# Attention scores of one sequence in six visits over four PSUM banks, value products in two cells, and one bank each for gate and up in the second half

## The chip, the cores and the metric

One NeuronCore of one Trainium2 chip runs the whole program. The metric is device time in microseconds (us) from the first to the last instruction of one execution; lower is better. Engines are named as the profile names them: PE (TensorE, matmul; PEld its weight loads), DVE (VectorE), ACT (ScalarE), POOL (GpSimd), SP (SyncE, which issues the DMAs).

## What is computed

Sixteen sequences of 256 tokens with 128 channels go through four residual blocks; all of it is fp32.

```python
x = L0_attn_a_x                                   # (16, 256, 128)
x = x + attn_a(layernorm(x))                      # linear attention: 32 heads of 4, a scan over tokens
x = x + ffn(layernorm(x))
x = x + attn_b(layernorm(x))                      # softmax attention, below
x = x + ffn(layernorm(x))                         # same weights again

def attn_b(x):                                    # 16 query heads of 8, one key and one value head
    q, k, v = x @ Wq + bq, x @ Wk + bk, x @ Wv + bv        # then rotary positions on q and k
    att = einsum('bthd,bThd->bhtT', q, k) / sqrt(8)
    att = softmax(where(causal, -inf, att))       # subtracts each row's maximum
    return einsum('bhtT,bThd->bthd', att, v).reshape(x.shape) @ Wo + bo

def ffn(x):                                       # sum over 8 experts, hidden width 512
    return sum(silu(x @ Wg[e]) * (x @ Wu[e]) @ Wd[e] for e in range(8))
```

## The kernel before

**Tiles, passes, units.** The 4096 tokens are 8 tiles of 512 (two sequences each). The feed-forward runs over all tiles twice, so there are 16 passes of 32 units, 512 units `n` in all. A unit is one expert's block of 128 hidden channels: `gate(n)`, `up(n)` and `down(n)` are three matmuls each of 512 columns (lines L855 to L857 of the helper `split_product`: high times high, high times low, low times high, in fp32r). ACT reads the gate bank (Silu in the units before `TANH` = 224, Tanh from there on, L684). From unit 224 on DVE then multiplies the gate into the tanh in `gated_half` (L1216, reads the gate bank again). DVE multiplies by the up bank in `hidden` (L1233), ACT rounds the product to HH (`hidden_hi`, L689), and POOL or DVE forms the rest HL (L525, L1222). `down(n)` runs three slots later and adds into one bank, `dbank`, for the 32 units of a pass.

**Slots.** Everything is placed on a common count of slots. In slot g PE runs gate(g), the side cells of point 0, up(g), the cells of point 1, down(g-3), the cells of point 2. The other engines walk over the same slots in program order: ACT does gate_act, hidden_hi of the slot before, then side work; DVE does gated_half, the maxima, a low part, hidden, then side work. Side work is the attention: block a for a tile is spread over some 48 slots beside the first half's passes, and block b (softmax attention) of tile t over 51 slots beside the second half's. In slots counted by `r` from a tile's first score visit, tile t's block b goes from r = -16 (its layer norm) to r = 35, and one tile follows the other every 32 slots, so that a lap of 32 slots holds each step of block b once. Where the unit does not exist (four slots between passes 8 and 9) only side work runs.

**Banks.** Before, three banks form a ring for gate and up (`fbank`: gate takes `2n % 3`, up `(2n+1) % 3`), `dbank` is one, two banks are `pair`, one is `single`, and `abank` takes block a's numerators and block b's value products. Tables `A_CELL` and `B_CELL` give each side cell its slot, point and bank. A cell waits until the cell that last used its bank has been read (`consumed`).

**Scores of one sequence.** Keys and queries are stacked in four row groups of 32 partitions (group g = 0 to 3), each with four heads j. First the row maxima: `rows`, six visits of two groups in the two banks of `pair`, with a matmul of 32 rows per group and head (L978, 128 columns; L987, 256 columns) and a causal mask added by a bf16 matmul into each bank (L981, L990); DVE reduces the two banks in one instruction (`maxima`, L1357, 128x1024). `split_maxima` (L1367, L1370) writes the maxima as weights, and `stack2` (L1074, L1076) adds them to the queries in the bank `single`; ACT copies it to Q2 (L804). Then `cols`, six visits with the transposed scores (L1005, or L1013 and L1021 with a wait between them, and masks L1008, L1017, L1024), which ACT turns into exponentials in PT, a ring of eight (`exps`, L766, 128x1024). `values` multiplies PT by v into `abank` in two halves of eight matmuls (L1035, L1041); ACT copies the result (L799), PE turns it (`sums`, L1050), DVE divides (L1379, L1382), and `ot` and `out` (L1057, L1065) project it.

The ring sets two waits in the second half, where PE may go one unit ahead:

```python
gate(n): after(pe, F.mul, n - 1)        # hidden(n-2) has read its up bank
up(n):   after(pe, F.sil, n); after(pe, F.half, n - TANH)   # gated_half(n-1) has read its gate bank
```

Of the kernel before, what the change touches and what calls it, by code (L numbers as in the profile page):

```python
# [14 lines left out]
P = 128  # L15
# [114 lines left out]
def unit_of(g):  # L130
# [17 lines left out]
for _b in range(SPT):
    for _i in range(6):
        B_CELL["rows", _b, _i] = (ROWS_AT[_b][_i], 0, None)  # L150
        B_CELL["cols", _b, _i] = (COLS_AT[_b][_i], 0, None)
BACK_CELL = (UNIT + LAG + 1, 2, 2)


def side_cells():
# [3 lines left out]
    def put(g, point, banks, key):  # L159
        for bank in (0, 1) if banks is None else (banks,):  # L160
            assert (g, point, bank) not in found, (g, point, bank, key)
            found[g, point, bank] = key
    for t in range(NT):
        for name, (r, point, bank) in A_CELL.items():
            put(a_slot(t) + r, point, bank, ("a", t, name))
        for name, (r, point, bank) in B_CELL.items():
            put(b_slot(t) + r, point, bank, ("b", t, name))
# [1369 lines left out]
```

## Time and profile before

| | us |
|---|---|
| median of 3 runs (lowest, highest) | 1717.82 (1716.12, 1718.82) |
| the profiled execution's own time | 1716.45 |
| its span, first to last instruction | 1714.7 |
| PE busy in it | 1574.8 (92%) |
| DVE, ACT, POOL busy | 1169.0, 892.6, 723.4 |
| passes 9 to 13 (one lap of block b each) | 113.0 each |
| pass 14 (end of the last tile's block b) | 100.1 |
| pass 15 (feed-forward alone) | 65.8 |

How to read it: a PE row's duration holds the time in which the matmul drains, so rows overlap, and the cost of a matmul is the distance between starts. A slot's length is the distance between the first gate matmuls of two units. "Idle before" is the time for which that engine had nothing to do, with what released it. PEclk is the share of full speed of TensorE's clock that was granted: 1.00 is 2.4 GHz, 0.50 is 1.2 GHz.

### The profile page before, as it was taken

What the parts mean: (1) busy time and instruction counts of PE and PEld (TensorE: products, weight loads), DVE (VectorE), ACT (ScalarE), POOL (GpSimd) and SP (SyncE); (2) the same over time, 40 slices, a digit from 0 to 9 for tenths busy, and PEclk for the clock granted to TensorE, in tenths of its full rate; (3) what the DMA queues carried; (4) which work ended last, traced back from release to release, by engine and by line L of the source; (5) the groups of instructions that cost most, each with busy time, mean ns of one, the idle gap of its engine ahead of it and who ended that gap; (6) DMA issues with size and microseconds to landing.
All of it is one profiled execution on the core that took longest, in us unless ns stands there. A gap on an engine that the chain in (4) does not pass through costs nothing.

```text
span 1714.7 us, 24047 instructions
## 1 busy us (share of the span) xinstructions
PE 1574.8 (92%) x7848; PEld 1136.2 (66%) x7848; DVE 1169.0 (68%) x1943; ACT 892.6 (52%) x1552; POOL 723.4 (42%) x663
## 2 busy tenths in 40 slices
PE   3488998899999999899999999999999999999998
PEld 2266777677767676675665766767667667576676
DVE  5678787878787869676674755746647557466465
ACT  2255555464646464546445564464554644645554
POOL 3647354534444434311033544444344444343365
PEclk9689999999999999999999999999999999999999
DMA  6314543333334434333222332422323323333353
GB/s 196 111 41 162 192 160 115 148 135 144 127 148 148 148 119 147 140 111 111 111 101 85 126 128 85 146 102 107 138 92 130 117 107 115 118 111 117 111 191 117
DMA packets 36239, 216.71 MB, mean 126 GB/s; under 512 B 3475, under 2 KB 17300, under 8 KB 19732
## 3 DMA queue, kind: packets, MB, share of 16 engines
q1 hardware_dynamic: 36116, 215.18, 34.7%
q8 instruction: 64, 1.05, 0.2%
q14 instruction: 59, 0.48, 0.1%
HBM read 200.49 MB, written 15.47 MB: 126 GB/s over the span
## 4 chain that ended last, share of the span: by engine, by line
issue 29%; POOL 20%; PE 1%; POOLq 0%; DVE 0%; ACT 0%; DVEq 0%
POOL HL L525 18%; POOL QK L597 1%; POOL X L588 0%; POOL RSTD_f L516 0%; POOL RSTD_in L516 0%; POOLq L190 0%; PE bank L855 0%; PE bank L857 0%; PE bank L856 0%; POOL VE_f L513 0%; POOL VE_in L513 0%; POOL NB_in L520 0%; POOL NM_f L518 0%; POOLq L196 0%; POOL NM_in L518 0%
## 5 line engine op out<-in xcount | busy, mean ns | idle before, releaser
L525 POOL TENSOR_TENSOR HL<-HF,HH 128x512 fp32r<-128x512 f32 x312 | 417.4, 1338 | 657.7 <-ACT HH L689 657.7
L1233 DVE TENSOR_TENSOR HF<-SG,bank 128x512 f32<-128x512 f32 x512 | 349.5, 683 | 172.7 <-PE bank L857 103.6
L855 PE MATMUL bank<-XTH,W 128*128 128x512 f32 x1024 | 434.4, 424 | 10.4 <-ACT SG L682 9.9
L857 PE MATMUL bank<-XTH,W 128*128 128x512 f32 x1024 | 403.8, 394 | 0.0
L1216 DVE SCALAR_TENSOR_TENSOR SG<-SG,bank 128x512 f32<-128x512 f32 x288 | 197.9, 687 | 301.3 <-ACT SG L684 300.6
L856 PE MATMUL bank<-XTL,W 128*128 128x512 f32 x1024 | 403.1, 394 | 0.0
L684 ACT ACTIVATE SG<-bank 128x512 f32<-128x512 f32 x288 | 172.3, 598 | 399.4 <-PE bank L857 397.8
L689 ACT ACTIVATE HH<-HF 128x512 fp32r<-128x512 f32 x512 | 319.7, 624 | 28.4 <-DVE HF L1233 27.6
L682 ACT ACTIVATE SG<-bank 128x512 f32<-128x512 f32 x224 | 133.6, 596 | 245.7 <-PE bank L857 244.4
L855 PEld LDWEIGHTS bank<-XTH,W 128*128 128x128 f32 x1024 | 194.8, 190 | 91.6 <-issue 29.8
L855 PE MATMUL bank<-HH,W 128*128 128x512 f32 x512 | 216.8, 423 | 14.6 <-DVE HL L1222 13.4
L857 PEld LDWEIGHTS bank<-XTH,W 128*128 128x128 f32 x1024 | 193.9, 189 | 43.6
L856 PEld LDWEIGHTS bank<-XTL,W 128*128 128x128 f32 x1024 | 195.1, 191 | 31.5
L857 PE MATMUL bank<-HH,W 128*128 128x512 f32 x512 | 202.5, 395 | 0.0
L856 PE MATMUL bank<-HL,W 128*128 128x512 f32 x512 | 201.5, 394 | 0.0
L1222 DVE TENSOR_TENSOR HL<-HF,HH 128x512 fp32r<-128x512 f32 x200 | 165.6, 828 | 0.0
L855 PEld LDWEIGHTS bank<-HH,W 128*128 128x128 f32 x512 | 97.2, 190 | 48.3 <-DVE HL L1222 16.8
L1357 DVE TENSOR_REDUCE NM<-pair 128x4 f32<-128x1024 f32 (+1 forms) x96 | 117.0, 1218 | 3.1 <-PE pair L981 2.1
L1269 DVE TENSOR_TENSOR_SCAN S<-BETA,KV 128x512 f32<-128x512 f32 x80 | 117.9, 1479 | 0.1
L857 PEld LDWEIGHTS bank<-HH,W 128*128 128x128 f32 x512 | 97.0, 189 | 22.2
L856 PEld LDWEIGHTS bank<-HL,W 128*128 128x128 f32 x512 | 97.4, 190 | 15.1
L562 POOL TENSOR_TENSOR S<-S,PQ 128x512 f32<-128x512 f32 x40 | 62.4, 1562 | 96.6 <-DVE S L1269 96.6
(237 smaller groups left out, 1850.0 us busy)
## 6 DMA issues: line engine op xcount, KB each, us to landing
W<-kept_w SPq DMA_DIRECT2D x120, 1536.0 KB, 6.5
kept_w<-W SPq DMA_DIRECT2D x8, 1536.0 KB, 6.2
X<-in_L_attn_a_x_dram SPq DMA_DIRECT2D x8, 256.0 KB, 5.5
WS<-in_L_ffn_Wg_dram SPq DMA_DIRECT2D x8, 256.0 KB, 6.5
WS<-in_L_ffn_Wu_dram SPq DMA_DIRECT2D x8, 256.0 KB, 6.8
WS<-in_L_ffn_Wd_dram SPq DMA_DIRECT2D x8, 256.0 KB, 7.2
out_dram<-X SPq DMA_DIRECT2D x8, 256.0 KB, 7.2
CST<-in_tables_dram SPq DMA_DIRECT2D x1, 896.5 KB, 5.2
```

The costliest lines, as they stand in the source:

```text
L525: g.tensor_tensor(HL[:, n % HRING, :], HF[:, n % HFRING, :], HH[:, n % HRING, :].bitcast(F32), ALU.subtract).then_inc(F.hl, 1)
L682: act.activation(SG[:, n % 2, :], fbank[2 * n % 3], ACT.Silu).then_inc(F.sil, 1)
L684: act.activation(SG[:, n % 2, :], fbank[2 * n % 3], ACT.Tanh, scale=0.5).then_inc(F.sil, 1)
L689: act.activation(HH[:, n % HRING, :], HF[:, n % HFRING, :], ACT.Copy).then_inc(F.hh, 1)
L855: pe.matmul(dst, wh, xh, start=start, stop=False)
L856: pe.matmul(dst, wh, xl, start=False, stop=False)
L857: return pe.matmul(dst, wl, xh, start=False, stop=stop)
L1216: v.scalar_tensor_tensor(gated, gated, 1.0, fbank[2 * n % 3], ALU.add, ALU.mult).then_inc(F.half, 1)
L1222: v.tensor_tensor(HL[:, n % HRING, :], HF[:, n % HFRING, :], HH[:, n % HRING, :].bitcast(F32), ALU.subtract).then_inc(F.hlv, 1)
L1233: v.tensor_tensor(HF[:, n % HFRING, :], gated, fbank[(2 * n + 1) % 3], ALU.mult).then_inc(F.mul, 1)
L1269: v.tensor_tensor_scan(S[:, m, c, :], BETA[:, m, :], KV[:, c, :], 0.0, ALU.mult, ALU.add).then_inc(A.scan, 1)
L1357: v.tensor_reduce(dst, src, AX.X, ALU.max, negate=True).then_inc(B.row_used, 1)
```

## The change

The eight PSUM banks are named anew: `gubank` (two), `quad` (four, next to each other), `dbank`, `abank`. In the first half the ring of three is kept (two banks of `gubank` and bank 0 of `quad`); from unit 224 on gate has one bank and up the other. A side cell may now lie in `quad` 0 to 3 or in `abank` (4). `rows` and `cols` make three visits per sequence each, all four groups at once, two slots apart and at point 2. Each visit ends with two pairs of masks, and signals after each pair; DVE takes one half (two banks) in the visit's slot and one in the next, ACT both halves in the next slot. `maxima` stands behind `hidden` in DVE's order. The value products of one head pair become one cell of sixteen matmuls. The stack goes from `single` to banks 0 and 1 of `quad`, both halves in one slot. Block b's layer norm starts five slots earlier (r = -21), and its turn is at r = -18.

```diff
-ROW_PAIRS = [(0, 1), (2, 3), (4, 6), (5, 7), (8, 10), (9, 11)]
-PT_RING = 8
-          ("stack", 0, 0): (8, 1, 2), ("stack", 0, 1): (9, 1, 2), ("stack", 1, 0): (14, 1, 2),
-          ("stack", 1, 1): (15, 1, 2), ("sums", 0, 0): (20, 1, 2), ("sums", 0, 1): (21, 1, 2),
-          ("ot", 0): (22, 1, 2), ("out", 0): (23, 1, 2), ("sums", 1, 0): (27, 1, 2), ("sums", 1, 1): (27, 2, 1),
-          ("ot", 1): (28, 1, 2), ("out", 1): (29, 1, 2), "fturn": (33, 2, 2)}
-ROWS_AT = [[6 * b + i for i in range(6)] for b in range(SPT)]
-COLS_AT = [[12 + 6 * b + i for i in range(6)] for b in range(SPT)]
+          ("stack", 0, 0): (7, 1, 0), ("stack", 0, 1): (7, 2, 1), ("stack", 1, 0): (13, 1, 0),
+          ("stack", 1, 1): (13, 2, 1), ("pv", 0, 0): (16, 1, 4), ("pv", 0, 1): (18, 1, 4), ("sums", 0, 0): (20, 1, 4),
+          ("sums", 0, 1): (21, 1, 4), ("pv", 1, 0): (22, 1, 4), ("pv", 1, 1): (24, 1, 4), ("ot", 0): (25, 1, 0),
+          ("out", 0): (26, 1, 0), ("sums", 1, 0): (26, 2, 4), ("sums", 1, 1): (27, 1, 0), ("ot", 1): (28, 1, 4),
+          ("out", 1): (29, 1, 4), "fturn": (33, 1, 4)}
+ROWS_AT = [[0, 2, 4], [6, 8, 10]]
+COLS_AT = [[12, 14, 16], [18, 20, 22]]
...
+        gubank = ctx.enter_context(nc.psum_tensor("gubank", [P, 2, 512], F32))[:, :, :]
+        quad = ctx.enter_context(nc.psum_tensor("quad", [P, 4, 512], F32))[:, :, :]
+        fbank = [gubank[:, 0, :], gubank[:, 1, :], quad[:, 0, :]]
+        sbank = [*[quad[:, i, :] for i in range(4)], abank]
+        def gate_bank(n):
+            return fbank[2 * n % 3] if n < TANH else fbank[0]
...
-            return {"rows": lambda: (B.row_used, 6 * n + name[2] + 1),
-                    "cols": lambda: (B.t_used, 6 * n + name[2] + 1),
+            return {"rows": lambda: (B.row_used, 6 * n + 2 * name[2] + 2),
+                    "cols": lambda: (B.t_used, 6 * n + 2 * name[2] + 2),
+                    "pv": lambda: (B.os, 2 * n + name[2] + 1),
...
             def exps(n, i):
-                m = 6 * n + i
-                act.wait_ge(B.t_ready, m + 1)
-                act.activation(PT[:, at:at + 2, :], pair, ACT.Exp, scale=DB ** -0.5).then_inc(B.t_used, 1)
+                for h in range(2):
+                    act.wait_ge(B.t_ready, 6 * n + 2 * i + h + 1)
+                    act.activation(PT[:, at:at + 2, :], quad[:, 2 * h:2 * h + 2, :], ACT.Exp,
+                                   scale=DB ** -0.5).then_inc(B.t_used, 1)
...
             def gate(n):
-                after(pe, F.mul, n - 1)
+                if n > TANH:
+                    pe.wait_ge(F.half, n - TANH)
+                else:
+                    after(pe, F.mul, n if n == TANH else n - 1)
             def up(n):
-                after(pe, F.sil, n)
-                after(pe, F.half, n - TANH)
+                if n > TANH:
+                    pe.wait_ge(F.mul, n)
+                else:
+                    after(pe, F.sil, n)
...
             def rows(t, b, i):
+                if i == 0:
+                    for j in range(NJ):
+                        for g in range(NG):
+                            pe.matmul(quad[:, g, j * P:(j + 1) * P], q[g][:, j, 0:P], ks[g][:, 0:P], start=(j == 0),
...
+                for h in range(2):
+                    for g in (2 * h, 2 * h + 1):
...
+                    m.then_inc(B.row_ready, 1)
...
+            def values(n, b, z, dst):
+                pe.wait_ge(B.t_used, 6 * n + 2 * z + 4)
...
             for slot in range(G_FIRST, G_LAST + 1):
-                for t, r in b_tiles(slot):
-                    for b in range(SPT):
-                        if r in ROWS_AT[b]:
-                            maxima(t, b, ROWS_AT[b].index(r))
...
                     hidden(n)
+                for t, r in b_tiles(slot):
+                    for b in range(SPT):
+                        for i, at in enumerate(ROWS_AT[b]):
+                            if r in (at, at + 1):
+                                maxima(SPT * t + b, b, i, r - at)
```

The places in the order of the instructions on which the prediction rests are three. In these rows `gubank`, `dbank` and `quad` (before: `bank`, `pair`, `single`) are banks, XTH and XTL the feed-forward's input, HH and HL its hidden product, QST, KST and Q_86 (Q2) the stacked queries and keys, NMP the maxima, PT the exponentials, and the names in brackets the semaphores waited for.

PE, slots r = 6 and 7 of a tile in the middle, the change: the first score visit of the second sequence at the end of slot 6, gate and up of slot 7, the first stack.

```order
L999 MATMUL quad<-KST,QST 128x128 [waits b_row_used]
L999 MATMUL quad<-KST,QST 128x128 x15
L1009 MATMUL quad<-MASKB 128x512 x4
L873 MATMUL gubank<-XTH,W 128x512 [waits f_half]
L874 MATMUL gubank<-XTL,W 128x512
L875 MATMUL gubank<-XTH,W 128x512
L873 MATMUL gubank<-XTH,W 128x512 [waits f_mul]
L874 MATMUL gubank<-XTL,W 128x512
L875 MATMUL gubank<-XTH,W 128x512
L1077 MATMUL quad<-QST,SELR 128x256 [waits b_nml,b_row_used]
L1079 MATMUL quad<-SELR,NMP 128x128 x2
```

The stack's bank is one that the score visit of the slot before filled, so the stack waits for `row_used`, the maxima of both halves. Before, the same place of PE (slot r = 8) had the stack in a bank of its own:

```order
L987 MATMUL pair<-KST,QST 128x256 [waits b_row_used]
L987 MATMUL pair<-KST,QST 128x256 x3
L990 MATMUL pair<-MASKB 128x2x128 x2
L855 MATMUL bank<-XTH,W 128x512 [waits f_half,f_sil]
L856 MATMUL bank<-XTL,W 128x512
L857 MATMUL bank<-XTH,W 128x512
L1074 MATMUL single<-QST,SELR 128x256 [waits b_nml,nf_lo]
L1076 MATMUL single<-SELR,NMP 128x128 x2
```

There the waits are for the split maxima and for a read that lies far back, and the score visit stands between gate and up instead of behind down.

ACT, slots r = 13 to 15 of the same tile, the change: the last instruction of hidden_hi in slot 13, then all side work of that slot and the next two.

```order
L707 ACTIVATE HH<-HF 128x512 [waits f_down,f_mul]
L783 ACTIVATE PT<-quad 128x1024 [waits b_pv,b_t_ready] x2
L822 ACTIVATE Q_86<-quad 128x512 [waits b_t_ready,b_q2_ready] x2
L693 ACTIVATE XN<-X,NB_in,RSTD_in 128x128 [waits nin_nb,nin_tp]
L693 ACTIVATE XN<-X,NB_in,RSTD_in 128x128 x3
L702 ACTIVATE SG<-gubank 128x512 [waits f_mul,f_gate]
L707 ACTIVATE HH<-HF 128x512 [waits f_down,f_mul]
L727 ACTIVATE XH<-abank 128x512 [waits b_v_ready,a_proj,nin_tp]
L702 ACTIVATE SG<-gubank 128x512 [waits f_mul,f_gate]
L707 ACTIVATE HH<-HF 128x512 [waits f_down,f_mul]
L783 ACTIVATE PT<-quad 128x1024 [waits b_pv,b_t_ready] x2
```

Two exponentials, two copies of the stack and the next tile's normalisation, which before were spread over the slots r = 12 to 18, stand in one slot now, ahead of the next slot's tanh (L702).

DVE, slots r = 11 and 12, the change: gated_half, hidden, the second half of the last maxima, the next tile's statistics, and the split of the second sequence's maxima.

```order
L1218 SCALAR_TENSOR_TENSOR SG<-SG,gubank 128x512 [waits f_sil]
L1235 TENSOR_TENSOR HF<-SG,gubank 128x512 [waits f_up,f_half,f_hl]
L1357 TENSOR_REDUCE NM<-quad 128x2x2 [waits b_row_ready,b_nml]
L1204 BN_STATS ST_in<-X 128x6 [waits nin_mv,f_done]
L1204 BN_STATS ST_in<-X 128x6 x3
L1208 BN_AGGR MV_in<-ST_in 128x2 [waits nin_nm,nin_st]
L1208 BN_AGGR MV_in<-ST_in 128x2 x3
L1218 SCALAR_TENSOR_TENSOR SG<-SG,gubank 128x512 [waits f_sil]
L1235 TENSOR_TENSOR HF<-SG,gubank 128x512 [waits f_up,f_half,f_hl]
L1367 CAST NMP<-NM 128x4x4 [waits b_q2_ready,b_row_used]
```

The maxima stand behind hidden, which itself waits for up of the same slot, and the statistics have come five slots forward to stand behind the maxima.

## Rows read from the trace of the kernel before

**Rows 1.** The page, part 1: busy time, share, instructions of PE and others
```profile
PE 1574.8 (92%) x7848; PEld 1136.2 (66%) x7848; DVE 1169.0 (68%) x1943; ACT 892.6 (52%) x1552; POOL 723.4 (42%) x663
```
**Rows 2.** Windows: a lap of block b, then pass 15; busy by engine, PEclk, DMA
```profile
1087.90:1200.90 113.00, 111.20 (x606) 75.83 (x604) 68.59 (x120) 60.59 (x105) 48.38 (x43) 1.00 0.32 115
...
1641.00:1706.80 65.80, 65.67 (x292) 54.03 (x290) 44.66 (x65) 36.29 (x66) 41.34 (x33) 1.00 0.45 164
```
**Rows 3.** Timeline of PE, three gates, two score visits between them (start, duration, engine, line)
```profile
1089.53 0.39 PE L855 MATMUL bank<-XTH,W 128*128 128x512 f32 x1
...
1090.30 0.50 PE L987 MATMUL pair<-KST,QST 32*128 32x256 f32 x4
...
1092.35 0.39 PE L855 MATMUL bank<-XTH,W 128*128 128x512 f32 x1
...
1095.54 0.39 PE L855 MATMUL bank<-XTH,W 128*128 128x512 f32 x1
```
**Rows 4.** Timeline of PE, around transposed scores (to 1119.89) and value products
```profile
1112.05 0.39 PE L855 MATMUL bank<-XTH,W 128*128 128x512 f32 x1
...
1114.87 0.39 PE L855 MATMUL bank<-XTH,W 128*128 128x512 f32 x1
...
1118.15 0.39 PE L857 MATMUL bank<-XTH,W 128*128 128x512 f32 x1
...
1119.89 0.39 PE L856 MATMUL bank<-XTL,W 128*128 128x512 f32 x1
...
1121.82 1.06 PE L1035 MATMUL abank<-PT,VF 128*32 128x512 f32 x8
...
1126.55 0.64 PE L1041 MATMUL abank<-PT,VF 128*32 128x256 f32 x8
```
**Rows 5.** Timeline of pass 15: a gate, its tanh, its gated_half, the next gate
```profile
1681.35 0.39 PE L855 MATMUL bank<-XTH,W 128*128 128x512 f32 x1
...
1682.23 0.60 ACT L684 ACTIVATE SG<-bank 128x512 f32<-128x512 f32 x1 [0.92 <-PE bank L857]
...
1682.86 0.69 DVE L1216 SCALAR_TENSOR_TENSOR SG<-SG,bank 128x512 f32<-128x512 f32 x1 [0.57 <-ACT SG L684]
...
1683.39 0.39 PE L855 MATMUL bank<-XTH,W 128*128 128x512 f32 x1
1683.64 0.69 DVE L1233 TENSOR_TENSOR HF<-SG,bank 128x512 f32<-128x512 f32 x1
```
**Rows 6.** Timeline of DVE: gated_half, maxima, hidden back to back
```profile
1093.86 0.69 DVE L1216 SCALAR_TENSOR_TENSOR SG<-SG,bank 128x512 f32<-128x512 f32 x1 [0.41 <-ACT SG L684]
1094.46 1.22 DVE L1357 TENSOR_REDUCE NM<-pair 128x8 f32<-128x1024 f32 x1
1095.60 0.68 DVE L1233 TENSOR_TENSOR HF<-SG,bank 128x512 f32<-128x512 f32 x1
```
**Rows 7.** Timeline of ACT: tanh, HH, an exponential; then one normalisation
```profile
1115.75 0.60 ACT L684 ACTIVATE SG<-bank 128x512 f32<-128x512 f32 x1 [0.79 <-PE bank L857]
1116.25 0.62 ACT L689 ACTIVATE HH<-HF 128x512 fp32r<-128x512 f32 x1
1116.77 1.02 ACT L766 ACTIVATE PT<-pair 128x1024 f32<-128x1024 f32 x1
...
1137.42 1.64 ACT L675 ACTIVATE XN<-X,NB_in,RSTD_in 128x128 f32<-128x128 f32 x4
```
**Rows 8.** Timeline: a product that had waited, DVE's ropes ahead of it
```profile
1165.84 1.40 DVE L1396 SCALAR_TENSOR_TENSOR B<-pair,BQK,CST 128x512 f32<-128x512 f32 x2
...
1166.64 0.50 PE L855 MATMUL pair<-XH,WBH 128*128 128x512 f32 x1 [0.77 <-DVE B L1396]
```
**Rows 9.** Timeline of PE in the first half, around two of its waits
```profile
633.38 0.50 PE L855 MATMUL bank<-XTH,W 128*128 128x512 f32 x1 [1.41 <-ACT SG L682]
...
635.52 0.63 PE L892 MATMUL single<-CST,XNF 128*128 128x128 f32 x4 [1.17 <-ACT XNF L675]
```
**Rows 10.** Windows of those waits; PEclk is the third number from the end
```profile
633.00:640.00 7.00, 5.46 (x18) 4.17 (x19) 3.85 (x7) 5.62 (x12) 0.29 (x2) 0.76 0.02 7
```

More of the change, by code:

```diff
@@ new lines, with back_cell, bank_of @@
+ROWS_AT = [[0, 2, 4], [6, 8, 10]]
+COLS_AT = [[12, 14, 16], [18, 20, 22]]
+for _b in range(SPT):
+    for _i in range(3):
+        B_CELL["rows", _b, _i] = (ROWS_AT[_b][_i], 2, None)
+        B_CELL["cols", _b, _i] = (COLS_AT[_b][_i], 2, None)
+BACK_CELL = (UNIT + LAG + 1, 2, 3)
+BACK_LATE = (UNIT + LAG + 1, 1, 4)
+def back_cell(s):
+    return BACK_CELL if s < NT - 2 else BACK_LATE
+def bank_of(key):
+    if key[0] == "back":
+        return back_cell(key[1])[2]
+    if key[0] == "a":
+        return A_CELL[key[2]][2]
+    if key[1:] == (0, "turn"):
+        return 3
+    return B_CELL[key[2]][2]
@@ L155, in side_cells, with put @@
 def side_cells():
     found = {}
[L159 to L162, printed above, removed]
+    def put(g, point, key):
+        bank = bank_of(key)
+        for at in range(4) if bank is None else (bank,):
+            assert (g, point, at) not in found, (g, point, at, key)
+            found[g, point, at] = key
     for t in range(NT):
[L164 to L167, printed above, removed]
+        for name, (r, point, _) in A_CELL.items():
+            put(a_slot(t) + r, point, ("a", t, name))
+        for name, (r, point, _) in B_CELL.items():
+            put(b_slot(t) + r, point, ("b", t, name))
@@ L983, in rows @@
                 else:
[L984 removed]
                     for j in range(2):
[L986 to L987 removed]
+                        for g in range(NG):
+                            pe.matmul(quad[:, g, j * SEQ:(j + 1) * SEQ], q[g][:, 2 * (i - 1) + j, P:SEQ], ks[g],
                                       start=(j == 0), stop=False, skip_group_check=True)
[L989 to L991 removed]
@@ new lines, in cols @@
+                for h in range(2):
+                    for g in (2 * h, 2 * h + 1):
+                        if i == 0:
+                            m = pe.matmul(r3(quad[:, g, :], NJ), MASKB[:, 2, :], spread(MASKB[:, 1, :], NJ),
+                                          start=False, stop=True, skip_group_check=True)
+                        else:
+                            m = pe.matmul(r3(quad[:, g, :], 2)[:, :, 0:P], MASKB[:, 2, :], spread(MASKB[:, 1, :], 2),
+                                          start=False, stop=True, skip_group_check=True)
+                    m.then_inc(B.t_ready, 1)
@@ new lines, in values @@
+            def values(n, b, z, dst):
+                pe.wait_ge(B.t_used, 6 * n + 2 * z + 4)
+                for g in range(NG):
+                    pe.matmul(dst[g * RG:(g + 1) * RG, :], VF[:, 2 * b, :], PT[:, NG * (z + 1) + g, :],
+                              start=True, stop=False, skip_group_check=True)
+                for g in range(NG):
+                    x = pe.matmul(r3(dst[g * RG:(g + 1) * RG, :], 2)[:, :, P:SEQ], VF[:, 2 * b + 1, :],
+                                  r3(PT[:, g, z * SEQ:(z + 1) * SEQ], 2), start=False, stop=True,
+                                  skip_group_check=True)
@@ L1132, in side @@
             def side(slot, point):
-                for t, r in b_tiles(slot):
-                    for b in range(SPT):
-                        for z in range(2):
-                            first = COLS_AT[b][3 * z + 2]
-                            if r in (first, first + 1) and point == 2:
-                                values(SPT * t + b, b, z, r > first)
                 for t, r in a_tiles(slot):
@@ L1481, in _ @@
                     gated_half(n)
-                for t, r in b_tiles(slot):
-                    for b in range(SPT):
-                        if r in ROWS_AT[b]:
-                            maxima(t, b, ROWS_AT[b].index(r))
                 old = unit_of(slot - 2)
```

234 lines of the change are left out of this document (91 added, 143 removed).

## The prediction

> **What bounds it now.** I read the page's busy times first, then the windows of single laps, then the timeline of PE inside a lap, because a mean over the span mixes the two halves. On the page PE leads with 92% [rows 1]. In a lap of block b it is busy for 111.2 of 113.0 us, while DVE has 68.6, ACT 60.6 and POOL 48.4 [rows 2]; the one long wait of PE is for DVE's ropes, 0.77 us in front of a product [rows 8], with a second like it. So in these laps PE's own work is the time, and in the last pass too (65.7 of 65.8). What is to be seen in the timelines is what a slot is made of. Without side work, gate to gate is 2.04 us [rows 5]: nine matmuls of 512 columns at 0.23. A slot with a small score visit (four matmuls of 256 columns, two masks) takes 2.82, with a large one (eight of 128 columns, two masks of 512) 3.19 [rows 3]. A first or second visit of the transposed scores gives 2.82 as well; the third takes 1.74 between two matmuls that are 0.45 apart without it, so 1.29 [rows 4]. A visit of 0.78 holds 0.23 of scores and 0.24 of masks; the other 0.3 is going into 32-row matmuls and out again.
>
> **What PE saves.** Per sequence the visits cost 2 x 1.15 + 4 x 0.78 = 5.4 for the maxima and 4 x 0.78 + 2 x 1.29 = 5.7 for the exponentials [rows 3, 4]. Four groups instead of two have no row. The two of a pair start together (the four instructions of the small visit occupy 0.50 in all [rows 3]), so the lower bound is that four cost what two do, plus two more masks; the upper is that the other two run after the first, 0.5 more per visit. I take the lower, since what is known is that groups of rows overlap, and keep the other for the range. Then the large visit is 1.15 + 2 x 0.23 = 1.6, the small 0.78 + 2 x 0.12 = 1.02, the first of the exponentials (four masks of 512) 0.78 - 0.24 + 4 x 0.23 = 1.45, the others 1.02: 3.6 and 3.5. The values' matmuls stay (1.06 and 0.64 per head pair [rows 4]); one cell for two saves one change of mode, 0.3, twice a sequence. Sum: 11.1 - 7.1 + 0.6 = 4.6 per sequence, 9.2 per lap.
>
> For this one step the Trainium skill has another figure: TensorE: Matmul & The Clock Gate, "Measured speedup vs the span model", gives four row tiles of 512 columns 3.07 times the speed of one, not four. By that, as an estimate, four would take 1.3 times as long as one, 0.1 to 0.15 more in each of 12 visits, some 12 us in the whole sum. No row here shows four groups at once.
>
> **What the ring of two adds.** A gate now waits for gated_half of the unit before. In pass 15 the tanh starts 0.88 after the gate's first matmul and gated_half 0.63 after that; it lasts 0.69 [rows 5]. So it ends 2.20 after the gate began, 0.16 later than the next gate begins today. A PE product released by DVE starts 0.05 after it and then takes 0.11 longer (0.50 instead of 0.39) because its weights load only then [rows 8]. So a slot without side work becomes 2.04 + 0.16 + 0.05 + 0.11 = 2.36. In pass 15 that is **32 x 0.32 = 10.3 us**, with no cover. Up waits for hidden, which starts 0.78 after gated_half and ends 0.73 after the gate it has released could start [rows 5]: about when PE gets there, so no further cost.
>
> **New waits in a lap**, counted from the gate's start in a slot; PE reaches the first side cell 1.36 after it (six matmuls).
> - Slot 7, stack behind the maxima of the visit one slot before. The tanh ends at 1.5, and until 1.6 DVE has the first half of these maxima, 1.13 to the next instruction [rows 6], and the split; gated_half and hidden follow (0.78 and 0.60 to the next instruction [rows 5, 6]), and the second half of the maxima, 1.22, ends at 4.2. PE waits **2.85**. Queued behind it are a down and the second stack, and with PE everyone.
> - Slot 13, stack behind two exponentials. Tanh starts at 0.88, HH 0.50 later, the exponentials 0.52 and 0.9 after that, and the second ends 1.02 later [rows 7], at 3.82. PE waits **2.5**.
> - Slot 14, turn of the next tile. ACT first copies two stacks (some 0.6 each, like the tanh), the second only when PE has made it, and then normalises for 1.64 [rows 7]: 2.35 after the slot's start against 1.36. **1.0**.
> - Slots 15 to 24. The value cells and the next q wait for exponentials that end at 3.82 of the slot before, or for the copy after them at 4.3; PE, after a short slot of 2.25, arrives at 3.7. Pair by pair the loss over PE's work is 0.5, 1.0, 0.35, 0 and 0.5: **2.3**.
> - Light slots 3, 5, 9 and 11, whose own gate did not wait, take 2.25 (no late weights) and push the next up by 0.1; DVE's extra work in slots 2, 8 and 11 delays three gates: **1.8**.
>
> Together 10.4. The two waits for ropes are partly filled, since out and sums now stand in slots 25 and 26 where PE idled: -1.4. A lap becomes 113.0 - 9.2 + 10.4 - 1.4 = 112.8. The 1.8 us that PE idled have become more than 10, and nothing is gained.
>
> **The rest.** The first lap (pass 7) has DVE form most of the low parts, 0.6 more per slot in front of hidden, and the gates now wait on DVE: +3. In pass 14, which has no next tile to prepare, the ten slots from 25 on are nearly bare and become up to 0.3 longer, less what the missing turn saves: +1.5. The change of rings at unit 224 costs one drained slot: +1. The first half keeps ring and places: 0. POOL's and SP's work is the same; the low parts have three slots of room and the weights load by passes. Six laps: -1. Sum: -1 + 3 + 1.5 + 1 + 10.3 = **+15**.
>
> **The clock.** The granted clock is 1.00 (2.4 GHz) in the lap and in pass 15 [rows 2]. In the first half PE waited 1.41 and then 1.17 us within 3.3 us [rows 9], and over 7 us the mean is 0.76 [rows 10], which is 3.4 us at 1.2 GHz; of six places like it three show this. Slots 7 and 13 with 14 wait longer than that, 16 times in all. If half of them bring such a stretch, each costs at most 1.7 us of PE's work: at most 14, and less behind slot 14, where ACT sets the pace. I take 7.
>
> Against the profiled execution's own 1716.45: 1716.45 + 15 + 7 = 1738.5, so **1738 us**; that execution lies 1.4 under the median of the runs, which is well inside the error. Its own range is 1724 to 1755: the laps' ten waits may each be off by some tenths, times seven laps, and the clock between 0 and 14.
>
> **Rivals.**
> - *PE's saving stays, the waits don't come* (faster). The place is the stacks and the turn in slots 7, 13 and 14, 6.3 us a lap. If DVE and ACT have read the banks when PE gets there, seven and a half laps lose 47 us less: 1691. For it: DVE idles 44 us of a lap, ACT 52 [rows 2]. Against it: both walk their queue in order, and the instruction waited for stands behind hidden or HH of the same slot. It decides at 2.8 us a lap: with less than 3.5 left of the 6.3 the change gains.
> - *Four groups don't overlap.* 12 visits x 0.5 x 7.5 laps = 45 at most; half of them hide in waits that exist anyway: +25, 1763. Against it the pairs that start together [rows 3].
> - *The clock falls at most of the 16 places, for longer.* Twice 14 instead of 7: 1759.
> - *It cancels*: pass 15 costs less than 10 and the laps gain 2 each: 1716 to 1721. That needs two errors of one sign.
>
> **Chances.** Forecast 0.52, PE's saving stays 0.19, no overlap 0.10, clock 0.10, cancels 0.09. A measurement of this kernel tells about 0.2%, 3.4 us, from no change. Faster by more 0.18, within it 0.09, slower 0.73. The range that leaves out 2 in 10 goes from 1700, which takes in the upper part of the first rival, to 1772.
>
> **What would show it.** Right: pass 15 near 76 us with gates 2.36 apart; PE's stack rows (L1077) with idle 2 to 3 us released by DVE's maxima (L1357) in slot 7 and by ACT's exponentials in slot 13; laps of 111 to 115. The four matmuls of a first exponential visit starting together, and taking no longer up to their masks than a pair did, would confirm the saving. Wrong: laps under 110 (waits absent), laps over 117 (groups in series, or PEclk well under 1.00 in the laps), or pass 15 still at 66.

## The result and the profile after

The changed kernel takes 1754.32 us (median; 1753.22 to 1765.98) against 1717.55 for the kernel before: ratio 1.022, 95% interval 1.0193 to 1.0247. It is slower by some 2%, as forecast (1738, range 1700 to 1772), and 16 us slower than the number given. The profiled execution took 1753.62, with a span of 1751.8, 37.1 over that of before.

The page of the changed kernel, part 1, answers to [rows 1]: PE has 17 us less to do in a span that is 37 us longer.

```profile
PE 1557.5 (89%) x7720; PEld 1115.4 (64%) x7720; DVE 1177.6 (67%) x1943; ACT 883.5 (50%) x1552; POOL 723.5 (41%) x663
```

Windows of the changed kernel: pass 7, pass 10 (a lap as in [rows 2]), pass 14, pass 15. Columns: stretch, length, busy time of PE, PEld, DVE, ACT, POOL, then PEclk, DMA share, GB/s.

```profile
740.80:870.60 129.80, 112.33 (x589) 75.81 (x589) 89.17 (x145) 59.99 (x102) 16.09 (x18) 0.96 0.28 101
1104.90:1219.70 114.80, 106.80 (x589) 73.61 (x587) 69.06 (x121) 59.39 (x104) 48.23 (x44) 0.99 0.31 115
1562.00:1667.20 105.20, 97.63 (x518) 65.79 (x516) 60.08 (x102) 53.81 (x92) 42.66 (x37) 0.98 0.33 119
1667.20:1743.90 76.70, 76.37 (x294) 49.70 (x292) 44.62 (x65) 36.37 (x65) 41.28 (x33) 1.00 0.38 140
```

The windows of passes 7 and 14 in the kernel before:

```profile
736.40:853.60 117.20, 113.30 (x603) 77.42 (x603) 82.44 (x145) 60.83 (x102) 16.08 (x17) 0.99 0.30 112
1540.90:1641.00 100.10, 99.32 (x532) 68.02 (x531) 58.36 (x101) 54.59 (x93) 42.62 (x36) 1.00 0.35 125
```

In the lap PE's idle time goes from 1.8 us [rows 2] to 8.0. The 37.1 us by passes, each from the end of the last `hidden` of one to that of the next: pass 0 +1.5, pass 6 +2.9, **pass 7 +12.6**, pass 8 -0.7, passes 9 to 13 together +4.9, pass 14 +5.1, **pass 15 +10.9**; passes 1 to 5 are equal within 0.1. Passes are counted from 0, so the four slots without a unit lie between passes 7 and 8. In the kernel before pass 13 takes 114.1 and not 113.0 like its neighbours, since a half-speed stretch of the clock stands in it (from 1513.3).

**The visits.** PE's timeline in the lap, around a large visit, a first visit of the exponentials, and a small one (start, duration, engine, line, count):

```profile
1094.24 0.39 PE L875 MATMUL dbank<-HH,W 128*128 128x512 f32 x1
1094.56 0.67 PE L999 MATMUL quad<-KST,QST 32*128 32x128 f32 x16
1095.16 1.04 PE L1009 MATMUL quad<-MASKB 128*128 128x512 bf16 x4
1095.85 0.59 PE L873 MATMUL gubank<-XTH,W 128*128 128x512 f32 x1
1096.27 0.39 PE L874 MATMUL gubank<-XTL,W 128*128 128x512 f32 x1
...
1135.31 0.51 PE L1025 MATMUL quad<-Q,KST 32*128 32x512 f32 x4
1135.74 1.04 PE L1029 MATMUL quad<-MASKB 128*128 128x512 bf16 x4
...
1146.16 0.40 PE L875 MATMUL dbank<-HH,W 128*128 128x512 f32 x1
1146.48 0.51 PE L1025 MATMUL quad<-Q,KST 32*128 32x512 f32 x4
1146.92 0.61 PE L1032 MATMUL quad<-MASKB 128*128 128x256 bf16 x4
1147.29 0.48 PE L873 MATMUL gubank<-XTH,W 128*128 128x512 f32 x1
1147.61 0.40 PE L874 MATMUL gubank<-XTL,W 128*128 128x512 f32 x1
```

From the last matmul of a down to the second of the next gate is 2.03 us over the large visit and 1.45 over the small, where two bare intervals of 0.227 would be 0.45: the visits cost 1.58 and 1.00 (predicted 1.6 and 1.02). The four matmuls of 512 columns start together and occupy 0.51, with the masks 0.43 behind their start. In the kernel before two of them had these same numbers:

```profile
1112.82 0.50 PE L1005 MATMUL pair<-Q,KST 32*128 32x512 f32 x2
1113.25 0.39 PE L1008 MATMUL pair<-MASKB 128*128 128x256 bf16 x2
```

**The stall in slot 7.** DVE, and then PE, in slots 6 and 7 of pass 10; the gate of slot 7 starts at 1113.28:

```profile
1113.31 1.22 DVE L1357 TENSOR_REDUCE NM<-quad 128x8 f32<-128x1024 f32 x1 [0.43 <-PE quad L1009]
1114.45 0.25 DVE L1367 CAST NMP<-NM 128x16 fp32r<-128x16 f32 x2
1114.73 0.29 DVE L1370 TENSOR_TENSOR NMP<-NM,NMP 128x16 fp32r<-128x16 f32 x2
1115.01 0.69 DVE L1218 SCALAR_TENSOR_TENSOR SG<-SG,gubank 128x512 f32<-128x512 f32 x1
1115.79 0.69 DVE L1235 TENSOR_TENSOR HF<-SG,gubank 128x512 f32<-128x512 f32 x1
1116.39 1.22 DVE L1357 TENSOR_REDUCE NM<-quad 128x8 f32<-128x1024 f32 x1
```

```profile
1117.66 0.39 PE L1077 MATMUL quad<-QST,SELR 128*128 128x256 f32 x1 [2.63 <-DVE NM L1357]
```

Read it downwards: first half of the maxima, split, gated_half, hidden, second half, and only then the stack. That is the queue the prediction wrote down, 0.2 us shorter. The three longest waits of PE in this lap (engine, tile, line, what it waited for; us, times, longest):

```profile
PE quad L1077 <- DVE NM L1357: 2.6, 1, 2.6
PE quad L1077 <- ACT PT L783: 2.3, 1, 2.3
PE abank L915 <- ACT XN L693: 0.9, 1, 0.9
```

**The ring of two.** The chain in pass 15, a gate, its tanh, its gated_half, the next gate, answers to [rows 5]:

```profile
1692.98 0.50 PE L873 MATMUL gubank<-XTH,W 128*128 128x512 f32 x1
...
1693.99 0.60 ACT L702 ACTIVATE SG<-gubank 128x512 f32<-128x512 f32 x1 [1.26 <-PE gubank L875]
...
1694.62 0.69 DVE L1218 SCALAR_TENSOR_TENSOR SG<-SG,gubank 128x512 f32<-128x512 f32 x1 [0.91 <-ACT SG L702]
...
1695.45 0.47 PE L873 MATMUL gubank<-XTH,W 128*128 128x512 f32 x1
```

Gates stand 2.47 apart here and 2.40 in the mean of the pass (2.36 predicted, 2.04 before).

**The clock.** Windows of the stall in slot 7 and of the stretch behind it (columns as above):

```profile
1114.00:1118.80 4.80, 2.17 (x13) 1.60 (x12) 3.48 (x8) 1.32 (x3) 1.27 (x1) 1.00 0.69 287
1118.80:1122.20 3.40, 3.40 (x13) 2.92 (x12) 0.00 (x0) 1.00 (x3) 0.00 (x0) 0.51 0.00 0
```

For 3.4 us the granted clock is 0.51 (the 1.2 GHz level). One such stretch stands in each of passes 9 to 14, in turn behind slot 13 and slot 7; pass 8 has both stalls and no stretch. That prices it, since the slots are otherwise alike: where it stands behind slot 7 the slots 7 and 8 take 7.28 and 4.29, without it 6.50 and 3.48, 1.6 together; where it stands behind slot 13 that slot takes 6.70 instead of 6.11, 0.6, and slot 14 no longer (4.57 for 4.54), as PE's wait of 0.86 for ACT falls away there. Passes 9 to 14 hold three of each: 6.6 us. Without them a lap is 113.2 us (predicted 112.8).

### The profile page after: what moved, and what is told of

Its sections match the earlier page's. It is cut to its first block and busy times, and to the rows that moved or that the text cites. A ratio compares the mean times of both kernels' runs of the same rounds, so it can differ in the third digit from the quotient of the medians.

```text
span 1751.8 us, 23526 instructions
## 1 busy us (share of the span) xinstructions
PE 1557.5 (89%) x7720; PEld 1115.4 (64%) x7720; DVE 1177.6 (67%) x1943; ACT 883.5 (50%) x1552; POOL 723.5 (41%) x663
## 3 DMA queue, kind: packets, MB, share of 16 engines
q8 instruction: 62, 1.02, 0.2%
## 5 line engine op out<-in xcount | busy, mean ns | idle before, releaser
L1218 DVE SCALAR_TENSOR_TENSOR SG<-SG,gubank 128x512 f32<-128x512 f32 x288 | 197.2, 685 | 349.3 <-ACT SG L702 349.0
L873 PE MATMUL gubank<-XTH,W 128*128 128x512 f32 x875 | 379.9, 434 | 26.2 <-DVE HF L1235 7.8
L702 ACT ACTIVATE SG<-gubank 128x512 f32<-128x512 f32 x288 | 172.9, 600 | 424.9 <-PE gubank L875 424.9
L1235 DVE TENSOR_TENSOR HF<-SG,gubank 128x512 f32<-128x512 f32 x438 | 300.0, 685 | 119.3 <-PE gubank L875 56.6
L874 PE MATMUL gubank<-XTL,W 128*128 128x512 f32 x875 | 347.8, 398 | 0.0
L875 PE MATMUL gubank<-XTH,W 128*128 128x512 f32 x875 | 347.6, 397 | 0.0
L873 PEld LDWEIGHTS gubank<-XTH,W 128*128 128x128 f32 x875 | 167.8, 192 | 132.0 <-DVE HF L1235 37.7
L873 PE MATMUL dbank<-HH,W 128*128 128x512 f32 x512 | 220.3, 430 | 12.9 <-DVE HL L1224 11.9
L875 PE MATMUL dbank<-HH,W 128*128 128x512 f32 x512 | 203.7, 398 | 0.0
L874 PE MATMUL dbank<-HL,W 128*128 128x512 f32 x512 | 202.4, 395 | 0.0
L875 PEld LDWEIGHTS gubank<-XTH,W 128*128 128x128 f32 x875 | 167.2, 191 | 38.3
L874 PEld LDWEIGHTS gubank<-XTL,W 128*128 128x128 f32 x875 | 168.4, 192 | 22.6
L700 ACT ACTIVATE SG<-gubank 128x512 f32<-128x512 f32 x149 | 88.9, 596 | 160.1 <-PE gubank L875 159.3
L873 PEld LDWEIGHTS dbank<-HH,W 128*128 128x128 f32 x512 | 97.5, 191 | 58.6 <-issue 26.0
L875 PEld LDWEIGHTS dbank<-HH,W 128*128 128x128 f32 x512 | 97.4, 190 | 22.1
```

Of the source, the lines that this page charges most:

```text
L700: act.activation(SG[:, n % 2, :], gate_bank(n), ACT.Silu).then_inc(F.sil, 1)
L702: act.activation(SG[:, n % 2, :], gate_bank(n), ACT.Tanh, scale=0.5).then_inc(F.sil, 1)
L873: pe.matmul(dst, wh, xh, start=start, stop=False)
L874: pe.matmul(dst, wh, xl, start=False, stop=False)
L875: return pe.matmul(dst, wl, xh, start=False, stop=stop)
L1218: v.scalar_tensor_tensor(gated, gated, 1.0, gate_bank(n), ALU.add, ALU.mult).then_inc(F.half, 1)
```

## The experiments

The theory is the prediction's: PE's saving is real, and the time is lost in waits that come from where the cells stand (stacks in the quad, the turn, one bank each for gate and up). The rivals: the stalls are slack of a chain through ACT and DVE; the clock is the loss; the order on DVE is of no account.

**e1_half_wait.** The stacks stand in banks 0 and 1, which the first half of a visit has read.

```diff
-                        after(pe, *consumed(old))
+                        sem, count = consumed(old)
+                        first = bank_of(key) in (0, 1) and old[0] == "b" and old[2][0] in ("rows", "cols")
+                        after(pe, sem, count - 1 if first else count)
```

> A stack in bank 0 or 1 of the quad waits only for the first half of the visit before it (first half of the maxima, first exponential), no longer for both halves. Theory (the two stacks' waits are the lap's loss): the idle time at L1077 in slot 7 goes from 2.63 to about 0.4 us (the split of the maxima of slot 6 is what is left), in slot 13 from 2.27 to about 1.25; 3.2 us a lap, eight laps, so 1754 - 26 = 1728; if the half-speed stretches, one a lap now, go with the shorter waits, up to 1.7 us a lap more, 1714. Rival (the chain through ACT and DVE sets the lap, PE's time in the stalls is slack): the time comes back in slots 8 to 12 and 14 to 24, 1746 to 1754. Second rival (the clock alone is the loss): waits shorter, but the gain is only where a half-speed stretch goes, at most 15 us, and laps without one keep 113 to 115 us.

Measured: **1712.28**, 0.9955 [0.9938, 0.9972] of before. The wait in slot 7 is 0.13, that in slot 13 as in this list of a lap's waits, with the lap's window:

```profile
PE quad L1077 <- ACT PT L783: 1.3, 1, 1.3
```

```profile
1084.80:1194.40 109.60, 105.04 (x589) 72.36 (x587) 69.05 (x122) 59.39 (x104) 48.25 (x44) 1.00 0.33 118
```

A lap gets 4.1 to 5.2 us shorter: 3.4 of waits, and the clock, which stays at 1.00 in passes 9 to 14. Over the profiled span of 1708.1 the laps of passes 9 to 13 give back 22.7 of 43.7 us, passes 6 and 7 another 10. The stalls were no slack, and the waits are the larger part; the clock goes with them.

**e2_stack_abank.**

```diff
-("stack", 0, 0): (7, 1, 0), ("stack", 0, 1): (7, 2, 1), ("stack", 1, 0): (13, 1, 0), ("stack", 1, 1): (13, 2, 1)
+("stack", 0, 0): (9, 1, 4), ("stack", 0, 1): (10, 1, 4), ("stack", 1, 0): (13, 1, 4), ("stack", 1, 1): (15, 1, 4)
```

> The four stacks move out of the quad into the fifth bank, to slots 9, 10, 13 and 15, so that they wait for no half of a visit. Theory (the stacks' place in the quad is the loss): 2.63 and 2.27 us a lap go, and up to 1 comes back, since the turn of the next tile in slot 14 and the stack in slot 15 now follow each other in one bank: 4 a lap, 32 in all, 1722; with the half-speed stretches gone too, 1707. Rival (ACT's and DVE's queues set the lap): 1745 or more, and the idle time shows up in front of the scores of slots 12 and 18 or the value products instead.

Measured: **1704.17**, 0.991 [0.9887, 0.9934], below what the theory gave even with the clock. The lap, and the longest wait left in it:

```profile
1086.50:1195.00 108.50, 104.52 (x589) 72.43 (x587) 69.03 (x122) 59.16 (x104) 48.29 (x44) 1.00 0.32 119
```

```profile
PE abank L915 <- ACT XN L693: 1.6, 1, 1.6
```

With the stacks elsewhere the quads beat the pairs by 4.5 us a lap (108.5 against 113.0). PE's waits in slots 7 and 13 are gone, and the turn in slot 14 takes 0.7 of it back.

**e3_ring_last.**

```diff
+            return ... fbank[0] if n < LAST else fbank[2 * (n - LAST) % 3]
...
-                if n > TANH:
+                if TANH < n <= LAST:
                     pe.wait_ge(F.half, n - TANH)
```

> From the last pass on, gate and up go round three banks again (the quad's first bank is the third). Theory (the chain gate, tanh, gated half, gate with one bank each costs 0.32 us a slot): the last pass falls from 76.7 to 66 to 67 us, 1754 - 10 = 1744, all other passes as they were. Rival (something else that came with the change, such as later low parts or weights, sets the last pass): 73 us or more there, 1750 to 1754.

Measured: **1748.14**, 1.0173 [1.014, 1.0206]. In the profile the last pass:

```profile
1668.20:1734.40 66.20, 66.10 (x294) 54.37 (x292) 44.63 (x65) 36.35 (x65) 41.32 (x33) 1.00 0.45 162
```

66.2 against 76.7, 65.8 before: all but 0.4 of pass 15's excess is the ring. The median gains 6 and not 10, with the four runs between 1744 and 1752. The profiled execution, the fastest of them, gains 9.5: there passes 13 and 14, which the edit does not touch, take 3.6 more, with a longer half-speed stretch in each, and pass 0 takes 2.4 less.

**e8_before_ring2.** The same from the other side: the kernel before, with gate and up in one bank each from the second half on, and the waits of the change for it.

```diff
-                after(pe, F.mul, n - 1)
+                if n > TANH:
+                    pe.wait_ge(F.half, n - TANH)
+                else:
+                    after(pe, F.mul, n if n == TANH else n - 1)
```

> The kernel before with one thing of the change: in the second half gate and up have one bank each, with the waits that this needs. Theory (the chain alone costs 0.32 us in each slot without side work, and little where a slot is 2.8 us or longer): the last pass goes from 65.8 to 76 us, a lap of block b by 0 to 3 us (up waits for the product, which there stands behind the maxima on DVE): 1728 to 1748, most likely 1732. Rival (the ring costs only together with the new places of the side work): last pass under 70, 1717 to 1722.

Measured: **1728.99**, 1.0061 [1.0046, 1.0076], 10 us more. The last pass:

```profile
1642.30:1719.00 76.70, 76.30 (x294) 49.69 (x292) 44.61 (x66) 36.37 (x65) 41.25 (x33) 1.00 0.38 141
```

10.9 there, 2.1 in pass 14, and 0.0 in the laps of passes 9 to 12, where each takes 113.0 as before. So with the side work where it was before, the chain costs only in slots that hold little but their unit.

**e4_pool_pass7.**

```diff
-            return n >= NT * UNIT or n % UNIT in POOL_LOW
+            return n >= TANH or n % UNIT in POOL_LOW
```

> In pass 7 all low parts are formed on POOL, as in the passes after it, instead of most of them on DVE. Theory (the 0.86 us low parts on DVE in front of the product make the gates and ups of pass 7 wait, and make its two stalls 4.1 and 3.7 instead of 2.6 and 2.3): pass 7 falls from 129.8 to 118 to 121 us, 1754 - 10 = 1744. Rival (pass 7 is long by its three half-speed stretches, 5 us, whatever DVE does): 125 us or more in pass 7, 1749 to 1754.

Measured: **1745.86**, 1.0153 [1.0124, 1.0182]. Pass 7 falls from 129.8 to 117.5. In the changed kernel its longest waits of PE are these:

```profile
PE gubank L873 <- DVE HF L1235: 7.2, 9, 1.3
PE quad L1077 <- DVE NM L1357: 4.1, 1, 4.1
PE quad L1077 <- ACT PT L783: 3.7, 1, 3.7
```

The nine for hidden become one of 1.3, and the 4.1 becomes 2.6. The 3.7 stays, against the theory: what makes it longer than the 2.3 of other laps is in the main a row of ACT, 1.28, that stands in front of its first exponentials and in no later lap:

```profile
796.53 1.28 ACT L783 ACT_TABLE_LOAD   x1
```

The kernel before has it too (at 776.88). Pass 8 takes 3.5 more, with two half-speed stretches that it did not have; the rest of the gain stays. The size fits, but the reason is not settled by it. The trace of the changed kernel shows what a wait of 1.28 is made of, POOL and DVE and then PE:

```profile
754.35 1.29 POOL L543 TENSOR_TENSOR HL<-HF,HH 128x512 fp32r<-128x512 f32 x1 [5.77 <-ACT HH L707]
754.39 1.79 DVE L1224 TENSOR_TENSOR HL<-HF,HH 128x512 fp32r<-128x512 f32 x1
...
756.10 0.67 DVE L1235 TENSOR_TENSOR HF<-SG,gubank 128x512 f32<-128x512 f32 x1
...
756.83 0.50 PE L873 MATMUL gubank<-XTH,W 128*128 128x512 f32 x1 [1.28 <-DVE HF L1235]
```

DVE's low part begins 0.04 after POOL's and lasts until 0.54 after POOL's has ended. Seven of DVE's 26 low parts in pass 7 are like this, 1.61 to 1.79 long; eighteen others take 0.68, and one 1.39, beside a sum of 128x512 on POOL (L615). The kernel before has one (1.81); six others begin there 1.17 behind POOL's and take 0.68. The next run takes POOL's away instead.

**e12_dve_pass7.**

```diff
-            return n >= NT * UNIT or n % UNIT in POOL_LOW
+            return n >= NT * UNIT or n < TANH and n % UNIT in POOL_LOW
```

> The opposite of the run with POOL's low parts: in pass 7 all low parts are formed on DVE, none on POOL. In the changed kernel's trace seven of DVE's 26 low parts in pass 7 take 1.6 to 1.8 us, each of them beside a low part on POOL that began within 0.3 us of it; eighteen of the other nineteen take 0.68. Theory (the two engines' low parts hold each other up, and the seven collisions are what makes pass 7 long): with none on POOL all take 0.68, though there are six more of them; the waits of 1.3 for the product go, and pass 7 falls from 129.8 to about 121, 1754 - 9 = 1745. Rival (DVE simply has too much to do in pass 7, and each low part in front of the product counts): six more low parts make it longer, 131 to 135, 1756 to 1759.

Measured: **1748.02**, 1.0163 [1.0134, 1.0192]. With 33 low parts on DVE instead of 26, pass 7 is 7.2 us **shorter** (122.6). The group of low parts on DVE in pass 7 (count, busy us, mean ns, idle before):

```profile
L1224 DVE TENSOR_TENSOR HL<-HF,HH 128x512 fp32r<-128x512 f32 x33 | 23.4, 710 | 0.0
```

The ten waits for hidden that are left are 0.2 each. Slot by slot, the five slots that had held such a wait lose 0.9 to 1.1 each and the two stalls 1.1 and 0.4. So 7.2 of pass 7's 12.6 is not DVE's amount of work, but that the two engines' low parts begin together. The amount is not free either: e4, where POOL forms them, has 117.5, and ten slots are some 0.4 shorter there than here. In each of the two steps, from the changed kernel to this run and from this run to e4, pass 7 also has 3.4 us less at half speed.

**e5_turn_back.** The turn goes back to `(-13, 1, 4)`, with statistics, normalisation and its two readers five slots later too.

> The next tile's normalisation and turn go back five slots later, to where the kernel before had them (turn in slot 19 of the lap, not 14), in the same bank; the stacks stay. Theory (the earlier normalisation costs 0.86 us in slot 14 and, for the first tile of block b, lands between block a's scans): pass 6 goes back from 95.8 to about 93, and the 0.86 in slot 14 goes; in slot 19 up to 1.0 comes, because the turn then follows the copy of the value cell of slot 18 in its bank: 1754 - 3 = 1751, at best 1744. Rival (the place of the turn is nothing): pass 6 stays at 95 to 96, 1754.

Measured: **1759.3**, 1.0233 [1.0209, 1.0256]: 5 us worse, where 3 to 10 better were expected. Pass 6 does fall, to 92.2. But the turn now follows the copy of a value cell in its bank, and the sums follow the turn and wait 0.3 for its copy (the first of these waits in pass 10):

```profile
PE abank L915 <- ACT OS L817: 1.0, 1, 1.0
```

1.3 for 0.9, and in passes 10, 11 and 14 twice the time at half speed, in pass 12 none. The expected 1.0 came; the second wait and the clock had been left out.

**e6_stack_turn.** From e2: turn at `(-17, 1, 4)`, stack (1, 1) at `(17, 1, 4)`.

> As the run with the stacks in the fifth bank, with the turn of the next tile one slot later (15, its normalisation still begun in 13) and the second sequence's second stack in slot 17. Theory (PE waits 1.59 us in slot 14 only because ACT has two exponentials and a stack's copy ahead of the normalisation): the wait goes, laps from 108.5 to about 107, 1704 - 11 = 1693. Rival (ACT is late for all of slots 13 to 18): the time comes back in front of the value products of slots 16 and 18 or of the scores of slot 18, 1700 to 1704.

Measured: **1736.98**, 1.0105 [1.009, 1.012], a miss by 44 us. The wait for XN is gone, and three others have come:

```profile
PE abank L1077 <- ACT OS L817: 2.8, 1, 2.8
PE gubank L873 <- DVE SG L1218: 1.4, 2, 1.0
PE abank L1040 <- DVE XL L1212: 1.0, 1, 1.0
```

The turn (15), a value cell (16), the stack (17) and a value cell (18) now follow each other in one bank, a slot apart. The value cell of 16 waits 1.0 for the turn's copy (XL), which the rival had; the stack of 17 waits 2.8 for the value cell's copy (OS), which ACT makes a slot later, behind that slot's unit. The lap is 112.9, with a half-speed stretch again. Neither theory had the 2.8. In e2 too the bank is used in the slots 13 to 16 running, but slot 17 behind the value cell is free: that was the slack.

**e7_all.** e6 with the edits of e3 and e4.

> The run before this one, with the ring of three in the last pass and POOL's low parts in pass 7. Theory (the costs lie in different passes and add up): 10.4 less in the last pass, about 6 less in passes 7 and 8 together, 1693 - 16 = 1677. Rival (POOL's low parts in pass 7 only push the cost into pass 8, where the run with that edit alone had 3.4 more): 1682 to 1690.

Measured: **1721.07**, 1.0011 [1.0, 1.0022]. It starts from e6's 1737, not from 1693, and ends where the kernel before stands, but the difference is what was expected, 15.9; in the profiles: 10.5 in pass 15 and 9.3 in pass 7, 1.4 given back in pass 8.

**e9_sum.** e2 with the edits of e3 and e4.

> The stacks in the fifth bank in slots 9, 10, 13 and 15, the ring of three in the last pass and POOL's low parts in pass 7, with the turn left in slot 14. Theory (the three costs lie in different passes and add up): 1704 - 10.4 (last pass) - 5 (pass 7, which still has 122 there against 117 before) = 1689, faster than the kernel before by 1.7%. Rival (POOL's low parts in pass 7 only move the time into pass 8): 1694.

Measured: **1688.92**, 0.9822 [0.9806, 0.9839]. The costs add up. Pass 7 is 112.8 (117.2 in the kernel before, 122.2 in e2), pass 15 66.2. Pass 8 gives 2.9 of pass 7's 9.4 back, as the rival had it for all of the 5.

**e10_norm_early.** From e9: statistics, scale and normalisation of the next tile one slot earlier (`r == -22`, `-21` and `-20`), the turn where it was.

> As the run with the sum, with the next tile's statistics, scale and normalisation one slot earlier (12 for ACT, which has no exponentials there), the turn still in slot 14. Theory (PE waits 1.59 us there for a normalisation that stands behind two exponentials and a copy on ACT): the wait goes down to about 0.3, which the copy of the stack in the same bank keeps; 1.3 a lap, 7 laps, 1689 - 9 = 1680. Rival (what is ahead of the turn in its bank is as late as the normalisation, or pass 6 gets longer by as much): 1687 to 1692.

Measured: **1676.61**, 0.9748 [0.9734, 0.9763], 2.5% faster than the kernel before. The wait for XN is gone; the statistics, now in DVE's slot 10, delay gated_half of slot 11 and with it the gate of slot 12 by 0.9, in the first row of the lap's waits:

```profile
PE gubank L875 <- DVE SG L1224: 1.6, 2, 0.9
```

So a lap gains only 0.8 to 1.0, some 4 of the 12 us in all. Passes 6 to 8 give 6, and lose three half-speed stretches (at 725, 790 and 862 us in e9); the rest is in passes 4 and 5, which the edit does not touch. That the number came out below the theory's 1680 is thus partly luck.

**e11_maxima_first.** The changed kernel with `maxima(...)` again ahead of `hidden_lo` and `hidden` in DVE's loop.

> The changed kernel with DVE's order of before: in each slot the maxima ahead of the low part and the product. Theory (with two banks the next up waits for the product, so the maxima of a visit that stands at the slot's end must be behind it): about 1.2 us more in each of the six slots after a visit of the maxima, 0.6 less at the stack of slot 7; 6 a lap, 1754 + 45 = 1799. Rival (the order on DVE is indifferent, since it idles 45 us a lap): 1750 to 1758.

Measured: **1788.93**, 1.0402 [1.0387, 1.0418]. A lap is 119.5, and among its waits are:

```profile
PE gubank L873 <- DVE HF L1235: 7.1, 8, 1.1
...
PE quad L1077 <- DVE NM L1357: 1.3, 1, 1.3
```

Eight ups wait 0.6 to 1.1 for hidden, and the stack in slot 7 waits 1.4 less. The order that the change gave DVE is part of what it needs, though DVE idles 45 us of a lap. In pass 7 it has a price: with the order of before only one of DVE's low parts begins together with POOL's (1.77 long), and four that begin 0.9 behind take 0.92; with the new one, in which the low part follows gated_half at once, seven begin together.

## Why the prediction was right, and where it was off

- **PE's saving: the visits right, the sum not shown.** 1.58 and 1.00 for visits predicted at 1.6 and 1.02, and four groups take no longer than two: 0.51 us for 0.50, with the masks 0.43 behind in both. But in a lap at full clock (e1) PE's busy time is 105.0, which is 6.2 less than before [rows 2] and not 9.2. The Trainium skill (TensorE: Matmul & The Clock Gate, "Measured speedup vs the span model") has four row tiles of 512 columns run 3.07 times as fast as one, not four times. No row here has one group alone, so this is neither confirmed nor refuted; from two groups to four no loss is seen.
- **New waits in a lap: the three long ones right in place and size.** 2.63, 2.27 and 0.86 in slots 7, 13 and 14 for 2.85, 2.5 and 1.0. e1 and e2 show that those at the stacks are the loss: with them shortened or gone laps are 109.6 and 108.5. The other two terms are smaller as idle time: 0.8 in slots 15 to 24 for 2.3, and 0.8 in front of the gates of slots 4, 10 and 12 for 1.8. So PE idles 8.0 us of a lap and not more than 10. That laps without the clock are 113.2 for 112.8 is then partly luck, since this and the smaller saving are two differences of about 3 of opposite sign. They may in part be one thing, as a wait shorter than a matmul's drain stands in a row's duration and not as idle time; this was not taken apart. Passes 8 to 13 come out at -0.8 for -1 without the clock of the changed kernel, 1.1 of it owed to the stretch in pass 13 of the kernel before.
- **Ring of two: right.** 10.9 for 10.3 in pass 15, shown by e3 and e8 from both sides. The +1 for the change of rings is not seen: PE does not idle at unit 224, and the first two slots of pass 7 are 5.9 us, 6.4 before.
- **Clock: right in number, a little low in size.** Eight of the 16 places bring a stretch: both of pass 7, none of pass 8, one in each of passes 9 to 14. The last six cost 6.6, where 7 was taken for all; pass 7's two are not priced. The stretches in pass 6 were not in the term.
- **The first lap: the step that failed.** "DVE form most of the low parts, 0.6 more per slot in front of hidden, and the gates now wait on DVE: +3" measured +12.6. What it left out is that the new order on DVE starts seven low parts at the moment POOL starts one, so that each takes 0.9 to 1.1 more than its 0.68. In five slots an up waits for that, and the stall in slot 7 grows to 4.1: 7.2 of the 12.6 go with POOL's low parts (e12). The term for the low parts themselves was too small as well: between e12, where DVE forms all, and e4, where POOL does, lie 5.1. The Trainium skill has the rule (SBUF — State Buffer, "SBUF: two separate sides": DVE and GpSimd lock one pair of ports for a whole instruction, for a DVE operation with two SBUF inputs beside a GpSimd operation that reads SBUF too, and the other engine waits). The trace agrees for the low parts: DVE's ended some 0.55 after the end of POOL's, whether it began 0.04 (1.79 long), 0.22 (1.61) or, in e11, 0.9 behind it (0.92).
- **Pass 14**: +5.1 for +1.5. 1.6 is a half-speed stretch, counted under the clock; the ring alone is 2.1 (e8). With the stacks' waits shortened (e1) the pass is back at 100.1; the rest is not taken apart.
- **"The first half keeps ring and places: 0"** missed pass 6, +2.9. There the first tile's normalisation, five slots earlier, falls among block a's last scans, and the turn waits 3.7 us for it. e5, which puts it back, has 92.2. But e1, with the same places and the same wait, has 93.4 and two stretches fewer, so most of the 2.9 is the clock.
- Pass 0 (+1.5) lies between 189.6 and 193.0 over the runs, with no edit there.

The rival "PE's saving stays, the waits don't come" was put at 1691. Its test is e2, where the stacks' waits are gone and the turn's is 1.6: 1704. That e9 lands at 1689 does not bear it out, since e9 also takes away the ring's cost in pass 15 and the low parts on DVE in pass 7.

## What to carry to other kernels

A bank that several engines read holds up whoever writes it next until the last of them has come round in its queue: put the next use behind a slot in which the readers can get there, or wait for just the half that was read. Fewer, larger visits save PE what they promise, and cost the slack that the small ones left between two uses of a bank; count both. When instructions that read two tensors in SBUF are reordered on DVE, see what POOL starts at the same moment.

## What the runs showed of the hardware

- Four 32-row matmuls of 512 columns, one on each group of rows, occupy PE for 0.51 us; two take 0.50.
- The clock does not follow a stall alone. In the changed kernel one of the two stalls of a lap (2.27 and 2.63) is followed by 3.4 us at the 1.2 GHz level, in turn. In e5, with the same two stalls, passes 10, 11 and 14 have twice that time at half speed and pass 12 none. In e11 a stall of 2.33 in slot 13 stands in the laps of passes 9 to 13 and PEclk is 1.00; in e6 a wait of 2.8 with two of 1.0 near it brings a stretch each lap. Why one and not the other was not settled.
- Two subtractions of 128x512 that begin within 0.3 us of each other on POOL and DVE: POOL's takes its usual 1.3, DVE's 1.61 to 1.79 instead of 0.68. The profile shows this as a longer DVE row and not as idle time. It does not meet every pair: `hidden`, which reads a bank of PSUM, takes 0.69 beside a low part of 1.30 on POOL (1693.02 and 1692.81), and a low part begun 0.13 behind a POOL operation of 128x4 that lasts 1.04 takes 0.68 (869.31, L534).
